# The first expert layer and the second attention of a two-layer transformer in another order: pooling from accumulated copies, selection moved behind other work, row sums by halves on GpSimd

## The reference, cut to what matters

```python
x = x + attn0(layernorm(x))       # 8 heads, scores 2048 x 2048, the largest part by far
x = x + ffn0(layernorm(x))        # first expert layer
x = x + attn1(layernorm(x))       # second attention, over 64 anchors
x = x + ffn1(layernorm(x))        # second expert layer
```

```python
def ffn0(x):                                      # x: [1, 2048, 128]
    pooled = x.mean(axis=1)                       # one mean over all 2048 rows
    gate = softmax(pooled @ gate_w.T)             # 8 experts
    top_w, top_i = top_k(gate, 2); top_w = top_w / (top_w.sum() + 1e-8)
    Wd, bd, Wu, bu = down_w[top_i], down_b[top_i], up_w[top_i], up_b[top_i]
    h = gelu(x @ Wd.T + bd) * top_w               # 2 experts of 64 hidden
    return h @ Wu.T + (top_w * bu).sum()

def attn1(x):                                     # 16 heads of 64, 64 anchors
    qk, v = split(x @ W_emb.T)
    attn = softmax(qk @ W_anchor.T * SCALE)       # per row and head, over 64 anchors
    out = (attn.T @ v) / attn.sum(rows)           # per head 64 x 64
    return (attn @ out) @ W_out.T + b_out
```

## Time and profile before

| | |
|---|---|
| median of 3 runs | 811.35 us (810.89 to 813.67) |
| the profiled execution | 810.39 us, span 808.6 us |
| PE / DVE / ACT / POOL busy in the span | 766.8 / 589.6 / 454.3 / 551.5 us |
| chain that ended last | PE 72%, DVE 10%, POOL 7%, issue 7%, ACT 3% |
| stages (us from the start) | first attention to about 538, first expert layer to about 575, second attention to about 684, second expert layer to the end |
| granted TensorE clock, mean | 0.984 of full speed |

### The profile page before, as it was taken

The page is one execution under the profiler, slowest core; times in us unless marked ns, Lnnn a source line. Parts: engine busy times, 40 slices in busy tenths (PEclk is TensorE's granted clock), DMA queues, the critical chain, the costliest instruction groups (busy, mean ns, idle before and its releaser), DMA issues.

```text
span 808.6 us, 12689 instructions
## 1 busy us (share of the span) xinstructions
PE 766.8 (95%) x4262; PEld 476.7 (59%) x4262; DVE 589.6 (73%) x1221; ACT 454.3 (56%) x1036; POOL 551.5 (68%) x472
## 2 busy tenths in 40 slices
PE   6899999999999999999999999989689889999997
PEld 4565555555555555555555554447455569888885
DVE  7777877877877877777777778763778815876564
ACT  3346666666666666666666655633666760445453
POOL 5058999998788788788788788932455471345554
PEclk9999999999999999999999999997999999999999
DMA  7100000000000000000000000012000000000000
GB/s 175 42 2 1 1 2 1 1 1 1 1 1 1 2 1 1 1 1 1 1 1 1 1 1 2 1 50 58 1 1 0 1 1 2 0 1 14 1 13 27
DMA packets 18761, 8.46 MB, mean 10 GB/s; under 512 B 8724, under 2 KB 17957, under 8 KB 18696
## 3 DMA queue, kind: packets, MB, share of 16 engines
q1 hardware_dynamic: 16230, 7.00, 3.4%
q10 hardware_dynamic: 2466, 0.66, 0.4%
HBM read 6.53 MB, written 1.05 MB: 9 GB/s over the span
## 4 chain that ended last, share of the span: by engine, by line
PE 72%; DVE 10%; POOL 7%; issue 7%; ACT 3%; POOLq 0%; DVEq 0%
PE ps L1334 20%; PE ps L1293 16%; PE ps L1279 14%; POOL hid_lo L855 6%; PE ps L1627 4%; PE ps L1316 3%; DVE mx L903 2%; PE ps L1611 2%; PE ps L1266 2%; DVE emb L1097 2%; DVE tmax L1093 1%; PE ps L1609 1%; PE ps L1594 1%; ACT pT L625 1%; ACT hT L619 1%
## 5 line engine op out<-in xcount | busy, mean ns | idle before, releaser
L903 DVE TENSOR_REDUCE mx<-ps 128x1 f32<-128x512 f32 x512 | 320.1, 682 | 90.7 <-PE ps L1279 90.6
L508 ACT ACTIVATE prob<-ps 128x512 f32<-128x512 f32 x512 | 267.9, 606 | 136.7 <-PE ps L1293 136.7
L795 POOL TENSOR_TENSOR part<-prob 128x512 f32<-128x512 f32 x189 | 241.2, 1284 | 52.0 <-PE ps L1341 45.7
L1293 PE MATMUL ps<-q_cols,key 128*128 128x512 f32 x512 | 215.2, 423 | 0.3 <-ACT prob L508 0.2
L1279 PE MATMUL ps<-key,q_rows 128*128 128x512 f32 x512 | 202.9, 400 | 4.6 <-DVE mx L903 2.5
L1341 PE MATMUL ps<-part,ones_v 128*32 128x512 f32 x384 | 183.1, 598 | 1.8 <-POOL part L795 1.1
L1334 PE MATMUL ps<-prob,val 128*32 128x512 f32 x1024 | 183.8, 599 | 0.0
L800 POOL TENSOR_TENSOR part<-part,prob 128x512 f32<-128x512 f32 x126 | 162.3, 1288 | 20.1 <-ACT prob L508 1.8
L1293 PEld LDWEIGHTS ps<-q_cols,key 128*128 128x128 f32 x512 | 95.8, 188 | 97.8 <-issue 75.3
L1279 PEld LDWEIGHTS ps<-key,q_rows 128*128 128x128 f32 x512 | 96.2, 189 | 30.1 <-DVE mx L903 13.3
L855 POOL TENSOR_TENSOR hid_lo<-hid,hid_hi 128x512 fp32r<-128x512 f32 x44 | 56.8, 1293 | 49.6 <-ACT hid_hi L664 49.6
(11 more groups left out here) (257 smaller groups left out, 1057.0 us busy)
## 6 DMA issues: line engine op xcount, KB each, us to landing
X<-in_L_attn_h_t_dram SPq DMA_DIRECT2D x4, 256.0 KB, 4.2
out_dram<-X SPq DMA_DIRECT2D x4, 256.0 KB, 2.3
w_raw<-in_L_ffn_w_g_dram SPq DMA_DIRECT2D x1, 704.0 KB, 4.4
w_raw<-in_L_ffn_w_u_dram SPq DMA_DIRECT2D x1, 704.0 KB, 6.1
w_raw<-in_L_ffn_w_d_dram SPq DMA_DIRECT2D x1, 704.0 KB, 7.9
w_o<-in_L_attn_W_O_dram ACTq DMA_DIRECT2D x1, 512.0 KB
w_out<-in_L_attn_W_out_dram SPq DMA_DIRECT2D x1, 512.0 KB, 4.7
q_cols<-nmx SPq DMA_DIRECT2D x32, 2.0 KB, 1.9
```

The costliest lines, as they stand in the source:

```text
L508: act.activation(prob[:, g % RING, :], ps[:, g % 3, :], ACT.Exp, scale=SCALE).then_inc(s_exp, 1)
L795: pool.tensor_tensor(total, p[0], p[1], ALU.add).then_inc(s_sum, 1)
L903: dve.tensor_reduce(mx[:, n % 2, c % TPB, at:at + 1], ps[:, pair(chunk_pair(lin)) + j, :], AX.X, ALU.max).then_inc(s_mrd, 1)
L1293: pe.matmul(ps[:, g % 3, :], key[:, n // NB % KBUF, t * P:(t + 1) * P], q_cols[:, n % NB, :], start=True, stop=True).then_inc(s_sc, 1)
```

## The change

What is done differently, in program order:

- End of the first attention: POOL's and DVE's last partial sums stand ahead of the normalisation of block 2 (`ln0_pool(2)`, `ln0_norm(2)`), and PE's transposes of block 1 ahead of the last `weighted` batches.
- Pooling: ACT's copies to `hT` also give their row sums (`accum_out`), DVE adds those of blocks 0 to 2, and PE sums only block 3 against ones; the 12 other one-column matmuls are gone. Logits come ahead of block 3's transposes.
- Both `anchor_weights` stand ahead of the last pooling, `values1(0)` is split around the pick, the bias of the hidden layer has 4 one-column products of its own, and the product for the up weights stands behind `hidden(0)`.
- `values1(1)` to `values1(3)` stand later, block 0 of the third normalisation is normalised by DVE, and the transposes use banks 5, 6, 7, 5.
- Second attention: ACT copies tile t-3 before the exponential of tile t; POOL adds the two halves of each row of 64 exponentials (`phalf`, over `sel` and `up_x`), and DVE sums 32 in place of 64, but for the last tile.
- After the loop: DVE copies half of `yT`, and `w_v`, `zz` and output go half by half.

```diff
-                out_hT = hT[:, b, :] if whole else hT_hi[:, b * BLK:(b + 1) * BLK]
-                act.copy(out_hT, ps[:, bank, :]).then_inc(s["hT"], 1)
+                if whole:
+                    act.activation(hT[:, b, :], ps[:, bank, :], ACT.Copy, accum_out=hsum[:, b:b + 1]).then_inc(s["hT"], 1)
+                else:
+                    act.copy(hT_hi[:, b * BLK:(b + 1) * BLK], ps[:, bank, :]).then_inc(s["hT"], 1)
             def on_vector_lo(dve, b, bank):
...
+                ln0_act(act, 1, 4)
                 sums(NBLK - 1)
-                ln0_act(act, 1, 4)
...
+                values1(1)
+                ln1_act(act, 0, T1_BANK[0])
+                ln1_norm(act, 1)
                 values1(2)
-                ln1_act(act, 0, 5)
-                ln1_norm(act, 1)
+                ln1_act(act, 1, T1_BANK[1])
+                ln1_norm(act, 2)
                 values1(3)
-                ln1_act(act, 1, 5)
-                ln1_norm(act, 2)
-                ln1_act(act, 2, 5)
+                ln1_act(act, 2, T1_BANK[2])
                 ln1_norm(act, 3)
...
                 for t in range(NT + LAG1):
                     if t == 1:
-                        ln1_act(act, 3, 5)
-                    if t < NT:
-                        act.wait_ge(s_cen, t + 1)
-                        if t >= 2:
-                            act.wait_ge(s_nr, t - 1)
-                        act.activation(prb[:, t % 2], cen[:, t % 2], ACT.Exp, scale=SCALE1).then_inc(s_pr, 1)
+                        ln1_act(act, 3, T1_BANK[3])
...
+                    if t < NT:
+                        act.wait_ge(s_cen, t + 1)
+                        if t >= 2:
+                            act.wait_ge(s_nr, t - 1)
+                        act.activation(prb[:, t % 2], cen[:, t % 2], ACT.Exp, scale=SCALE1).then_inc(s_pr, 1)
                 act.wait_ge(s_y_ps, NT)
...
+                for t in range(NT + 1):
+                    if t < NT - 1:
+                        pool.wait_ge(s_pr, t + 1)
+                        if t >= 2:
+                            pool.wait_ge(s_ts, t - 1)
+                        pool.tensor_tensor(phalf[t % 2], prb[:, t % 2, :, 0:A // 2], prb[:, t % 2, :, A // 2:A], ALU.add).then_inc(s_half, 1)
+                    if t >= 1:
+                        u = t - 1
+                        pool.wait_ge(s_tr, u + 1)
+                        if u >= 3:
+                            pool.wait_ge(s_y_ps, u - 2)
+                        pool.tensor_tensor(nrm[u % 3][:, :, :], prb[:, u % 2],
+                                           trec[:, u % 2, :].unsqueeze(2).to_broadcast([P, H1, A]), ALU.mult).then_inc(s_nr, 1)
...
+                last_sums(2)
                 ln0_norm(dve, 2)
-                last_sums(2)
                 accumulate(NBLK - 1, 1)
                 ln0_stats(dve, 3)
+                dve.wait_ge(ln0["hT"], NB + 3)
+                dve.tensor_reduce(hsum[:, NB:NB + 1], hsum[:, 0:NB - 1], AX.X, ALU.add).then_inc(s_pooled, 1)
                 ln0_norm(dve, 3)
                 dve.wait_ge(s_pool_ps, 1)
-                dve.tensor_copy(pooled[:, :], ps[:, 0, AT_POOL:AT_POOL + 1]).then_inc(s_pooled, 1)
+                dve.wait_ge(s_pooled, 1)
+                dve.tensor_tensor(pooled[:, :], ps[:, 0, AT_POOL:AT_POOL + 1], hsum[:, NB:NB + 1], ALU.add).then_inc(s_pooled, 1)
...
-                        dve.wait_ge(s_pr, u + 1)
-                        dve.tensor_reduce(tsum[:, u % 2, :], prb[:, u % 2], AX.X, ALU.add).then_inc(s_ts, 1)
+                        if u < NT - 1:
+                            dve.wait_ge(s_half, u + 1)
+                            summed = phalf[u % 2]
+                        else:
+                            dve.wait_ge(s_pr, u + 1)
+                            summed = prb[:, u % 2]
+                        dve.tensor_reduce(tsum[:, u % 2, :], summed, AX.X, ALU.add).then_inc(s_ts, 1)
                         dve.wait_ge(s_ts, u + 1)
                         if u >= 2:
                             dve.wait_ge(s_nr, u - 1)
...
+                dve.wait_ge(s_yh, 1)
+                dve.tensor_copy(yT[:, 0:BLK], ps[:, 4, :]).then_inc(s_yT0, 1)
...
-                dve.wait_ge(s_z_ps, 1)
                 for m in range(2):
+                    dve.wait_ge(s_z_ps, m + 1)
...
+                        if n == NBLK - 1 and slot == 7:
+                            ln0_pe(pe, 1, 4)
                 for w in range(1, NW):
                     weighted(NBLK - 1, w)
-                ln0_pe(pe, 1, 4)
...
-                def pool_rows(b):
-                    for t in range(TPB * b, TPB * (b + 1)):
-                        last = pe.matmul(ps[:, 0, AT_POOL:AT_POOL + 1], hn[:, t, :], ones_v[:, 0:1], start=(t == 0), stop=(t == NT - 1))
-                    return last
...
-                pe.wait_ge(ln0["hn"], 2 * NT)
-                pool_rows(NB - 1).then_inc(s_pool_ps, 1)
-                pe.wait_ge(ln0["hT"], NB + 2)
-                ln0_pe(pe, 3, 4)
-                pe.wait_ge(s_pooled, 1)
-                pe.matmul(ps[0:1, 0, AT_LOGIT:AT_LOGIT + E], pooled[:, :], gate0T[:, :], start=True, stop=True).then_inc(s_lg, 1)
...
+                pe.wait_ge(s_an, 3)
+                anchor_weights(0)
+                anchor_weights(1)
+                pe.wait_ge(ln0["hn"], 2 * NT)
+                for t in range(NT - TPB, NT):
+                    last = pe.matmul(ps[:, 0, AT_POOL:AT_POOL + 1], hn[:, t, :], ones_v[:, 0:1], start=(t == NT - TPB), stop=(t == NT - 1))
+                last.then_inc(s_pool_ps, 1)
+                pe.wait_ge(s_pooled, 2)
+                pe.matmul(ps[0:1, 0, AT_LOGIT:AT_LOGIT + E], pooled[:, :], gate0T[:, :], start=True, stop=True).then_inc(s_lg, 1)
+                pe.wait_ge(ln0["hT"], NB + 2)
+                ln0_pe(pe, 3, 4)
+                pe.wait_ge(s_wo, 2)
+                value(0, 0)
+                value(0, 1)
...
                 def ln1_T(b):
-                    pe.wait_ge(s_wa_lo, 2)
-                    if b >= 1:
-                        pe.wait_ge(ln1["lo"], b)
-                    ln1_pe(pe, b, 5)
-                anchor_weights(0)
+                    if b == 0:
+                        pe.wait_ge(s_wa_lo, 2)
+                    elif b < 3:
+                        pe.wait_ge(s_h0, b + 2)
+                    else:
+                        pe.wait_ge(ln1["lo"], 1)
+                    ln1_pe(pe, b, T1_BANK[b])
...
-                values1(0)
+                value(0, 2)
+                value(0, 3).then_inc(s_wv_ps, 1)
                 pe.wait_ge(ln0["hT"], NB + 3)
                 pe.wait_ge(s_pick, 1)
...
+                    last = pe.matmul(ps[:, 2, D:D + 1], masks[j], down0_b[:, j:j + 1], start=(j == 0), stop=(j == E // 2 - 1))
                 last.then_inc(s_su_ps, 1)
                 pe.wait_ge(s_sdT, 1)
                 hidden(0)
                 pe.wait_ge(s_gv, 10)
+                pe.matmul(ps[0:E, 0, AT_GB:AT_GB + P], g8[:, IDX, :], ones_row[:, :], start=True, stop=True).then_inc(s_gb_ps, 1)
                 pe.wait_ge(s_selb, 1)
+                pe.wait_ge(s_upx, 1)
+                for j in range(E // 2):
+                    last = pe.matmul(ps[:, 2, 0:D], masks[j], up_x[:, j, :], start=(j == 0), stop=(j == E // 2 - 1))
...
+                hidden(1)
                 pe.wait_ge(s_gbc, 1)
                 pe.matmul(ps[:, 0, AT_BIAS:AT_BIAS + D], gb[:, :], up0_b[:, :], start=True, stop=True).then_inc(s_b0_ps, 1)
-                hidden(1)
                 pe.wait_ge(s_suT, 1)
                 up(0)
-                values1(1)
                 hidden(2)
                 up(1)
+                hidden(3)
+                values1(1)
+                up(2)
+                ln1_T(0)
+                up(3)
                 values1(2)
-                hidden(3)
-                ln1_T(0)
-                up(2)
-                values1(3)
                 ln1_T(1)
-                up(3)
...
+                    if t == 1:
+                        values1(3)
+                        pe.wait_ge(s_wv, 4)
+                    elif t in (2, 3):
                         ln1_T(t)
...
+                            if u == NT - 1 and m == 0:
+                                last.then_inc(s_yh, 1)
                         last.then_inc(s_y_ps, 1)
-                pe.wait_ge(s_yT, 2)
                 for h in range(H1):
+                    if h % 8 == 0:
+                        pe.wait_ge(s_yT0 if h == 0 else s_yT, 1)
                     half = slice((h % 2) * A, (h % 2 + 1) * A)
                     hp = h // 2
                     last = pe.matmul(ps[half, hp // 4, (hp % 4) * P:(hp % 4 + 1) * P], yT[:, h * A:(h + 1) * A], w_v[:, h, :],
                                      start=True, stop=True)
-                last.then_inc(s_z_ps, 1)
-                pe.wait_ge(s_z, 2)
+                    if h % 8 == 7:
+                        last.then_inc(s_z_ps, 1)
                 def output1(b, i):
                     if b >= 2 and i == 0:
```

(2 more changed lines are left out.)

161 lines of the change are left out of this document (78 added, 83 removed).

## The result

The changed kernel takes 802.89 us (median of 4 runs, 802.56 to 803.14) where the kernel before takes 811.12 (4 runs, 810.54 to 813.67): ratio 0.9892, 95% interval 0.9871 to 0.9914. Another set of runs gave 803.08 (801.53 to 803.66), ratio 0.9883 (0.9863 to 0.9904). It is faster by 8.2 us, within the range given; the forecast of 798.5 was 4.4 us too low. The profiled execution took 803.11 us.

A forecast was written before the change was run, and what follows sets the result against it. PE was taken as the bound wherever it has work, its waits being what can shrink. With the clock falling, 3.7 + 0.3 + 6.0 + 2.7 = 12.7 us off the median 811.35 gave about 798.5 us, range 792 to 804.5.

The forecast's parts named there:

- second, pooling to logits: Expert layer, last normalisation to logits: eight one-column products, addition and logits take about 1.4 us, not 2.9; -1.5 us.
- third step: Logits to the down product: anchor products leave the chain, 2.5 us with handovers in place of 4.3; -1.8 us.
- fourth step: Down product to the first gelu: 0 if PE runs at half clock, -2.9 us at whole clock.
- fifth step: Gelu to first addition to X: later up product and bias chain cost +1.4 us, +0.5 at whole clock, +2.4 at half.
- sixth step: First addition to X to the loop's first transposes: earlier normalisation and longer queues nearly cancel; -0.3 us, +-1.5.
- seventh step: Second attention's loop: old ring opened, 4.33 us a turn; first to last transposes 61.5 us, not 67.54; -6.0 us.
- The ring through POOL: Second attention's loop: exponential, half sum, product, next exponential close a turn of 4.33 us, longer than PE's 3.98.
- rival (a): Expert selection: PE's clock does not fall, the layer gives 7.5 in place of 3.7 us; 794.8 us, chance 0.27.
- Rival (b): Loop: half sums slower on short pieces, 1.90 us each, a turn 4.95 us; 806.6 us, chance 0.10.
- (d): Loop: opening the old ring gains nothing because PE waits elsewhere, for instance on late exponentials; 804.5 us, chance 0.09.
- (c): Loop: POOL's half sum held up beyond 2.44 us, making the kernel slower; 813 us or more, chance 0.03.
- The sentence on the rule of the Trainium skill: Loop: element-wise additions belong on VectorE; without half sums it would run at PE's 3.98 us, 4.5 us sooner.

The follow-up runs named there:

- experiment 4: Kernel before with only ACT's order changed in the second attention's loop (copies of tile t-3 ahead of the exponential of tile t): 800.93 us, ratio 0.9862.
- experiment 5: Kernel before with only the half sums on POOL added, exponential still ahead of the copies: 810.92 us, ratio 0.9989.
- experiment 2: Changed kernel with ACT's exponential ahead of the copies of tile t-3 again, half sums kept: 805.95 us, ratio 0.9924.
- experiment 6: Changed kernel with four wide products, results unused, in one piece ahead of the last pooling: 803.73 us, ratio 0.9879.
- experiment 8: Changed kernel with the accumulated copies undone, PE pooling all tiles against ones, 24 one-column products ahead of the anchor products: 800.45 us, ratio 0.9852.
- experiment 7: Changed kernel with four wide products, results unused, spread from the last pooling to the masks' products: 797.75 us, ratio 0.9818.
- experiment 10: Changed kernel without half sums and with four unused wide products spread through the selection: 792.72 us, ratio 0.9761.
- experiment 11: Changed kernel without half sums, with four unused wide products spread through the selection and the bias product early: 791.39 us, ratio 0.9735.
- experiment 1: Changed kernel without the half sums, DVE summing all 64 exponentials of a row: 795.63 us, ratio 0.980.
- experiment 9: Changed kernel with the bias product ahead of the second hidden product and ACT's copy of it ahead of the up weights' scaling: 802.05 us, ratio 0.9869.

## Why the prediction was right or wrong, by its steps

In the sum the profile was to end 12.7 us sooner; it ended 7.2 sooner. The steps, each counted on the profiled executions (predicted, measured):

| step | predicted | measured |
|---|---|---|
| start to the mark | 0 | +2.4 |
| first, end of the first attention | -1.85 | -1.9 |
| second, pooling to logits | -1.5 | -1.5 |
| third, logits to the down product | -1.8 | -0.7 |
| fourth, down product to the first gelu | 0 | 0.0 |
| fifth, gelu to the first addition to X | +1.4 | +2.8 |
| sixth, to the loop's first transposes | -0.3 | -0.4 |
| seventh, the loop | -6.0 | -5.3 |
| eighth, the tail | -2.7 | -2.7 |

**What was right.** The ring through POOL, its length (4.33 forecast, 4.37 measured), the half sum (1.28 taken, 1.27 measured) and that it sets the pace: taking it out leaves 3.75 to 3.99. The 0.7 us that the seventh step falls short is 0.04 a turn and the first and last tiles. The clock falls in the selection, and rival (a) didn't come. Rival (b) falls with the half sum's 1.27 us, (d) with experiment 4 and (c) with the time itself.

The sentence on the rule of the Trainium skill (GPSIMD Engine Reference, section 4.1 "Engine selection") also held, and more strongly than I let it. The same addition of two 128x512 tiles takes 1.28 us on POOL and 0.69 on DVE (at 533.03 and 535.61 in the changed kernel), 1.9 times as long. The loop without half sums runs 5.25 us sooner, not 4.5, and the kernel 7.3 us. In experiment 5, in the other order, it gains nothing. In neither order of ACT's queue did the half sum on POOL pay.

**Right in part by luck.** That the seventh step came out at -5.3 is not all the pace. In the kernel before one turn stands out:

```profile
593.22 1.06 ACT L619 ACTIVATE hT<-emb 128x1024 f32<-128x1024 f32 x1 [0.63 <-DVE emb L1097]
...
600.11 1.06 ACT L619 ACTIVATE hT<-emb 128x1024 f32<-128x1024 f32 x1 [3.77 <-DVE emb L1097]
```

```profile
592.00:596.00 4.00, 4.00 (x13) 2.27 (x10) 2.57 (x3) 3.37 (x21) 2.15 (x2) 0.57 0.00 0
```

It takes 6.89 us, with the clock at half from 592.0 to 595.4; the ten turns behind it take 3.98 and 4.98 by turns. So some 1.9 of the 67.54 us are a fall of the clock that the changed kernel's profile doesn't have in its loop. The steady pace, 4.48 before and 4.37 after, gives only about 1.1 us in these ten turns. Taken apart, the 5.3 us are 2.2 from the first exponential to the last (65.26 and 63.08 us, the fall of the clock included), 2.2 from the last exponential to the transposes of tile 15 (7.45 and 5.21), which is due to the order on ACT (experiment 2 has 7.45 again), and 0.8 because the first transposes come later behind the first exponential (5.17 and 6.01), which the sixth step pays. The prediction had worked out only the changed kernel's 61.5 us and taken the difference.

**What failed.** The third step: "with handovers 2.5 us" was worked out from durations at whole clock, while I had forecast a clock that falls "from about 545". At half clock the same chain took 3.55 us, from 547.15 to 550.70; in experiments 6 and 8, where the clock was still whole for nearly all of it, it took 2.31. I kept the fall for the fourth step and forgot it in the third.

The fifth step: "+1.4 if it rises after the hidden layer has begun". The clock rose 3.7 us after the first gelu, so 3.7 of the 6.1 us of this stretch ran at half, where I had put the low stretch at 7 to 10 us and it lasted 13.7. And the bias chain costs more than I had put: even at whole clock, in experiments 7 and 10, gelu to the addition is 4.3 us, +1.0 and not +0.5; experiment 11 has 3.5 with the bias product early. So of the +2.8, 1.0 is the longer chain and 1.8 the clock; even the upper bound of +2.4 was too low.

The start: no step of the prediction had it. The mark is at 530.8 to 531.7 in the three profiles of kernels with the old first part (before, experiments 4 and 5), and at 531.6 to 533.8, 532.9 in the mean, in eleven of kernels with the changed program. The instructions up to there are the same. What differs in the profiles is small and early: in seven of the eleven PE waits 0.2 to 0.8 us at about 9.5 us for the transfer of `uk`, in none of the three; and from 76 us on the distance stays as it is (the first addition of a head's result to X is at 74.17 before, 76.53 after). The four of the eleven without that wait come 0.4 to 2.1 us behind the mean of the three (531.2) all the same. The clock goes with a part of it: it is low for 3.4 us once or twice ahead of 56 us in every profile, and where the last of these stretches lies at 51 to 56 us (five of the eleven) the mark is at 533.3 to 533.8, where it lies at 41 to 49 (the other six, and the three) at 531.6 to 532.9 and 530.8 to 531.7. Why the start comes later stays open; no run here separates the causes.

**What the change is worth, taken apart.** The order on ACT brings about 10 us (experiment 4). The half sums take 7.3 of it back (experiment 1). The new order of the expert layer and the tail bring about 5 (795.63 against 800.93), although the clock still falls; without the fall they bring 3 to 5 more (experiments 10 and 7). Of the layer's parts, the accumulated copies cost about 2 (experiment 8).

## What to carry to other kernels

When an operation is handed to an engine with spare time, first write out every ring that this engine closes: here an engine that was busy 71% of the span, and 3.2 of the 4.37 us of a turn, set the pace, because two of its operations and one of another's stood in one turn, and the sum of their durations, not its load, was the price. Where an order is opened and a load is moved in one change, time each by itself; the one can be worth more than both. And in a chain of small steps, taking work out of PE while it waits is no gain: price the whole chain at one clock level, and look at what PE does ahead of the fall before removing anything there.

## What the hardware showed that I had not expected

- The same 24 one-column products (2.74 us) stood ahead of an early fall in one order and of a late one in another. In the place of the wait of 1.68 us they let the clock stay whole 3.4 us longer, from the mark, and it was low half as long (experiment 8). In the kernel before it fell at 544.2, 0.8 us behind them, while PE was busy with eight transposes (543.30) and had been busy in all of the 6.2 us ahead. The wait of 0.79 us there came after the fall, not ahead of it as the prediction reads these rows. Four wide products that compute nothing put the fall off by 3.3 us in one piece (experiment 6), and spread they kept the clock whole for the entire selection (experiment 7). What decides besides the wait stays open.
- Lengths of the low stretch of the selection in these profiles: 13.7 us before and after, 10.2 in experiment 6, 6.8 in experiment 8, 17.1 in experiment 9, none in experiments 7, 10 and 11. In the changed kernel and in experiment 9 it stayed low although PE was busy all the time from 547 to 560.
- POOL's addition of 512 elements a partition takes 1.27 us whether it reads whole rows or halves of rows of 64; so the short pieces cost nothing.
